# State-space prelude: both batches' x-projections before z, convolution taps read from PSUM, diagonals of both batches through DRAM, -|x| and an expert-block residual on VectorE

## What is computed

```
h = layernorm(x) * (1 + ca) + sa
xs, z = split(h @ in_proj.T)                       # 512 + 512 channels
xa = silu(conv4(xs) + conv_b)                      # causal, 4 taps
dt, Bc, Cc = split(xa @ x_proj.T)                  # 16 + 16 + 16
dt = softplus(dt @ dt_proj.T + dt_b)
for t: h_t = h_t-1 * exp(dt * A) + dt * B_t * xa   # 16 states a channel
       y_t = sum_n h_t[n] * C_t[n]
y = (y + xa * D) * silu(z)
x = x + ga * (y @ out_proj.T)
...
# layer 1, as the reference has it: the inner block adds its own input h
x = x + gb * (h + moe(rmsnorm(h)))
```

## Time and profile before

| | |
|---|---|
| Three runs, us | 2557.56, 2559.26, 2559.46; median 2559.26 |
| Profiled execution | 2562.03 us; its span 2560.2, granted clock of TensorE 0.957 of 2.4 GHz on average |
| TensorE, VectorE, ACT, POOL busy | 91%, 55%, 44%, 45% of the span |
| `mamba` begins | 34.7 us |
| First and last scan begin | 179.8, 530.1 us |
| `moe` of layer 1 begins | 2248.7 us |

### The profile page before, as it was taken

How to read it: one execution, slowest core, us unless ns; L and a number is a source line. 1 busy time by engine, 2 the same in 40 slices (tenths; PEclk the granted TensorE clock), 3 DMA queues, 4 the chain that set the end, 5 groups by cost and what they waited for, 6 DMA issues and landing times. The chain is left out here.

```text
span 2560.2 us, 34038 instructions
## 1 busy us (share of the span) xinstructions
PE 2337.4 (91%) x12526; PEld 1769.7 (69%) x12526; DVE 1416.2 (55%) x2477; ACT 1120.5 (44%) x1913; POOL 1140.2 (45%) x665
## 2 busy tenths in 40 slices
PE   6959999985999995999998989999999999949997
PEld 2329999983777764998896667777776777725554
DVE  5658888866222223545665875556556555463332
ACT  3467777722111112434433555546456464521221
POOL 0439999920332321433454445454545535223442
PEclk8969999997999997999998999999999999969999
DMA  6274181118412212000000100000000001055223
GB/s 243 83 284 114 58 329 59 64 73 267 133 30 34 32 26 98 1 1 1 1 1 19 56 1 19 15 10 19 1 23 1 19 9 34 1 175 145 45 42 64
DMA packets 108244, 168.30 MB, mean 66 GB/s; under 512 B 30482, under 2 KB 77586, under 8 KB 106004
## 3 DMA queue, kind: packets, MB, share of 16 engines
q1 hardware_dynamic: 93108, 145.35, 16.3%
q0 software_dynamic: 14976, 20.78, 5.1%
HBM read 115.94 MB, written 52.32 MB: 66 GB/s over the span
## 5 line engine op out<-in xcount | busy, mean ns | idle before, releaser
L638 POOL TENSOR_TENSOR mb_dbx<-mb_ud,mb_bb 128x1024 f32<-128x1024 f32 x128 | 302.0, 2363 | 57.2 <-DVE mb_h L496 41.7
L496 DVE TENSOR_TENSOR_SCAN mb_h<-ps,mb_dbx 128x1024 f32<-128x1024 f32 x128 | 292.2, 2289 | 47.9 <-ACT ps L608 37.5
L2298 PE MATMUL ps<-a_eT,a_v 128*128 128x512 f32 x576 | 297.2, 598 | 3.9 <-ACT a_eT L2175 3.9
L2131 POOL TENSOR_TENSOR a_e<-a_e,a_rc 128x1024 f32<-128x1024 f32 (+5 forms) x144 | 188.9, 1321 | 248.3 <-DVE a_rc L2047 247.9
L946 POOL DMA_INDIRECT e_acc<-e_hid,e_ids x78 | 123.6, 1585 | 370.8 <-DVE e_hid L1240 354.4
L2057 DVE TENSOR_REDUCE a_mx<-ps 128x1 f32<-128x1024 f32 (+7 forms) x256 | 192.7, 753 | 159.1 <-PE ps L2277 158.3
L2175 ACT ACTIVATE a_eT<-ps 128x512 f32<-128x512 f32 x288 | 171.1, 594 | 245.3 <-PE ps L2288 244.6
L740 PE MATMUL ps<-mb_dg,mb_hts 128*128 128x128 f32 x2048 | 251.2, 276 | 0.4
L740 PEld LDWEIGHTS ps<-mb_dg,mb_hts 128*128 128x128 f32 x2048 | 240.0, 193 | 1.9 <-issue 1.9
L1226 DVE COPY e_work<-ps 128x256 f32<-128x256 f32 x78 | 33.2, 425 | 356.4 <-PE ps L1064 356.4
L1803 POOL TENSOR_TENSOR a_elo<-a_e,a_ehi 128x1024 fp32r<-128x1024 f32 x48 | 117.6, 2451 | 223.2 <-ACT a_ehi L1656 117.7
(11 more groups left out here) (377 smaller groups left out, 5310.9 us busy)
## 6 DMA issues: line engine op xcount, KB each, us to landing
mb_bb<-mb_db_rows SPq DMA_DIRECT2D x16, 1024.0 KB, 12.6
mb_ddiag<-mb_dg SPq DMA_DIRECT2D x1, 8192.0 KB, 22.3
mb_dg<-mb_ddiag SPq DMA_DIRECT2D x8, 1024.0 KB, 14.0
e_wg<-in_g SPq DMA_DIRECT2D x8, 688.0 KB, 10.4
e_wu<-in_u SPq DMA_DIRECT2D x8, 688.0 KB, 10.7
e_wd<-in_d SPq DMA_DIRECT2D x8, 640.0 KB, 10.7
mb_dxa<-mb_bb SPq DMA_DIRECT2D x8, 512.0 KB, 2.6
mb_dz<-mb_xz SPq DMA_DIRECT2D x8, 512.0 KB, 2.9
```

Of the source, the lines that this page charges most:

```text
L496: dve.tensor_tensor_scan(h[:, at % 2, :], pair(at % 2), dbx[:, at % 2, :], 0.0, ALU.mult, ALU.add).then_inc(s_h, 1)
L638: pool.tensor_tensor(dbx[:, at % 2, :], ud[:, kk % 2, 0, :], bb[:, n, :], ALU.mult).then_inc(s_dbx, 1)
L2131: pool.tensor_tensor(probs(i, h), probs(i, h), rc[:, q:q + 1].to_broadcast([P, (i + 1) * P]), ALU.mult).then_inc(s["en"], 1)
L2298: mm = pe.matmul(ps[:, 6 + rows[u, i] % 2, :], v[:, j, u % 2, :], eT[:, k % ER, :], start=(j == 0), stop=(j == i))
```

## The change

In `mamba`:

- The order is now all eight x products (with `narrow` and `steps` as soon as they can), and only then all eight z products (`gated`, `gate`).
- `normalised` writes (x - mean) * rstd only, to two buffers. Scale and shift of the modulation go into the eviction to `hT`: TensorE transposes the 8 modulation blocks (`columns`, new), VectorE copies 8 columns to `modT`, ACT's Identity takes them as scale and bias.
- The zero-padded copy `xp` is gone. ACT's last tap and VectorE's three other taps read the product in PSUM, a tap that lies d tokens back over L - d elements.
- |v| is gone from ACT. VectorE computes relu r = max(v + b, 0) and then v - 2 r in a second pass; ACT's Exp adds the bias, which gives exp(-|v + b|).
- The step sizes and u of group 0 are made in `ud` itself, where the first scans read them.
- POOL builds no diagonals. `place_words` and `load_diag` run for both batches; SP issues batch 0's placements between the x spills.
- z is put in `xz`, `dbx`, `h` and again `xz`. So POOL's first product waits for the spill of z 2 and 3 (`s_zout[1]`), the first scan for z 4 and 5 (`s_zout[2]`), gate 6 for z 0 and 1.

In `moe` of layer 1, the four residual operations move from POOL to VectorE, behind the sixteen normalised tiles and the small constants and ahead of the wait for the router.

The core of the diff:

```diff
+        two = lambda area: area.rearrange("p a (t d) -> p (a t) d", d=D)
+        xn = [two(dg[:, 0:2, :]), two(dg[:, 4:6, :])]
+        hT = [dg[:, 2:4, :], bb[:, 12:14, :]]
+        zr = [xz[:, 0, :], xz[:, 1, :], dbx[:, 0, :], dbx[:, 1, :], h[:, 0, :], h[:, 1, :], xz[:, 0, :], xz[:, 1, :]]
...
             def load_ud(kk):
-                if kk >= 2:
+                if kk == 1:
+                    sp.wait_ge(s_low, BK)
+                    sp.wait_ge(s_uout[0], 16 * (CD - 1))
+                    sp.wait_ge(s_dtout[0], 16 * (CD - 1))
+                else:
...
+            for k in range(CD):
+                spill_xa(0, k)
+            spill_xa(1, 0)
+            spill_rows(0)
+            spill_xa(1, 1)
+            place_words(0)
+            spill_xa(1, 2)
+            spill_xa(1, 3)
+            sp.wait_ge(s_tr, 4)
+            sp.wait_ge(s_dgout, 16 * TB)
+            load_diag(0, 0)
+            spill_rows(1)
+            for k in range(1, CD):
+                spill_steps(0, k)
+                spill_z(k - 1)
+            spill_z(CD - 1)
...
             def conv(i):
...
+                    late = DC - 1 - tap
+                    ins = dve.scalar_tensor_tensor(xc[:, i % 2, late:L], pair(PAIR["x"][i])[:, 0:L - late], cw[:, k, tap:tap + 1],
+                                                   xc[:, i % 2, late:L], ALU.mult, ALU.add)
...
+            def relu(i):
+                dve.wait_ge(s_dt, i + 1)
+                own(dve.tensor_scalar(dtv[i // CD][i % CD], pair(PAIR["dt"][i]), db[:, i % CD:i % CD + 1], 0.0, ALU.add, ALU.max))
+                dve.scalar_tensor_tensor(low_v[i // CD][i % CD], dtv[i // CD][i % CD], -2.0, pair(PAIR["dt"][i]),
+                                         ALU.mult, ALU.add).then_inc(s_low, 1)
...
             for at in range(NIT):
                 kk, n = at // NS, at % NS
                 dve.wait_ge(s_da, at + 1)
                 dve.wait_ge(s_dbx, at + 1)
+                if at == 0:
+                    dve.wait_ge(s_zout[2], 32)
...
+            falling(0)
+            falling(1)
+            log1p(0)
+            for i in range(CD):
+                gate(i)
             log1p(1)
+            for i in range(CD, BK):
+                gate(i)
...
             pool.memset(zeros, 0.0).then_inc(s_zero, 1)
-            pool.wait_ge(s_ct, 1)
-            for n in range(NS):
-                if n == 12:
-                    pool.wait_ge(s_sp, CD)
-                pool.tensor_tensor(dg[:, n, :].rearrange("p (q c) -> p q c", q=TB), over(ident[:, :], TB),
-                                   spread(ct[:, n::NS], P), ALU.mult).then_inc(s_dg, 1)
             for at in range(NIT):
                 kk, n = at // NS, at % NS
-                if n == 0:
-                    pool.wait_ge(s_ud[kk % 2], 32 * (kk // 2 + 1))
+                if at == 0:
+                    pool.wait_ge(s_u, 1)
+                    pool.wait_ge(s_zout[1], 32)
...
+            columns()
             turned(0)
...
+            inner(0)
+            inner(1)
+            inner(2)
             turned(1)
+            inner(3)
+            inner(4)
+            narrow(0, 0)
+            narrow(0, 1)
+            inner(5)
+            narrow(0, 2)
+            narrow(0, 3)
+            inner(6)
+            steps(0)
...
+            for i in range(CD, BK):
+                steps(i)
+            for i in range(BK):
+                gated(i)
...
         def _(pool):
-            if hs is not None:
-                for r in range(NG // B, NG):
...
+            if hs is not None:
+                for r in range(NG // B, NG):
+                    four = slice(4 * r, 4 * r + 4)
+                    own(dve.tensor_tensor(res[:, four, :], hs[:, four, :],
+                                          over(mod[:, r // (NG // B), GB * D:(GB + 1) * D], 4), ALU.mult))
+                    ins = dve.tensor_tensor(x[:, four, :], x[:, four, :], res[:, four, :], ALU.add)
+                ins.then_inc(s_res, 1)
```

More of the change, by code:

```diff
@@ L473, in _ @@
-            relu(0, CD - 1)
-            split_xd(1)
-            for k in range(CD):
-                steps(0, k)
-            for k in range(CD):
-                relu(1, k)
-            for k in range(CD):
-                steps(1, k)
+            for i in range(6):
+                conv(i)
+            relu(0)
+            conv(6)
+            relu(1)
+            conv(7)
+            relu(2)
+            relu(3)
+            dve.wait_ge(s_dbl, 2)
+            dve.tensor_copy(xd[1], flat(ps[0:80, 2 * PAIR["narrow"][1]:2 * PAIR["narrow"][1] + 2, :])).then_inc(s_xd, 1)
@@ L555, in absolute @@
-            def absolute(b, k):
-                act.wait_ge(s_relu, b * CD + k + 1)
-                if b == 0 and k == 0:
-                    act.wait_ge(s_zfill, 16)
-                if b == 1 and k == 0:
-                    act.wait_ge(s_uout[0], 16 * CD)
-                act.activation(abs_v[b][:, k, :], pair(dt_pair(b, k)), ACT.Abs, bias=db[:, k:k + 1]).then_inc(s_abs, 1)
-            def falling(b):
-                for k in range(CD):
-                    act.wait_ge(s_abs, b * CD + k + 1)
-                    act.activation(abs_v[b][:, k, :], abs_v[b][:, k, :], ACT.Exp, scale=-1.0).then_inc(s_exp, 1)
@@ L582, in _, with activated @@
-            inner(1, 0)
-            for k in range(1, CD):
-                inner(1, k)
-                activated(1, k - 1)
-                absolute(0, k - 1)
-            activated(1, CD - 1)
-            gates(1, 0)
-            absolute(0, CD - 1)
+                act.activation(xc[:, i % 2, :], pair(PAIR["x"][i]), ACT.Identity, bias=cb[:, k:k + 1],
+                               scale=cw[:, k, DC - 1:DC]).then_inc(s_tap, 1)
+            def activated(i):
+                act.wait_ge(s_conv, i + 1)
+                act.activation(xa[i // CD][i % CD], xc[:, i % 2, :], ACT.Silu).then_inc(s_xa, 1)
@@ new lines, in falling, with log1p @@
+            def falling(b):
+                for i in range(b * CD, (b + 1) * CD):
+                    act.wait_ge(s_low, i + 1)
+                    act.activation(low_v[b][i % CD], low_v[b][i % CD], ACT.Exp, bias=db[:, i % CD:i % CD + 1]).then_inc(s_exp, 1)
+            def log1p(b):
+                for i in range(b * CD, (b + 1) * CD):
+                    act.wait_ge(s_exp, i + 1)
+                    act.activation(low_v[b][i % CD], low_v[b][i % CD], ACT.Ln, bias=1.0).then_inc(s_log, 1)
@@ new lines, in gate @@
+            def gate(i):
+                act.wait_ge(s_ip, BK + i + 1)
+                if i == 0:
+                    act.wait_ge(s_zfill, 16)
+                    act.wait_ge(s_xa, BK)
+                if i == 6:
+                    act.wait_ge(s_zout[0], 32)
+                act.activation(zr[i], pair(PAIR["z"][i]), ACT.Silu).then_inc(s_z, 1)
+            rows_of(0)
+            tap(0)
+            tap(1)
+            activated(0)
+            tap(2)
+            rows_of(1)
+            activated(1)
@@ L590, in _ @@
+            tap(3)
+            activated(2)
+            tap(4)
+            activated(3)
+            tap(5)
+            activated(4)
+            act.wait_ge(s_dbl, 1)
+            act.activation(xd[0], flat(ps[0:80, 2 * PAIR["narrow"][0]:2 * PAIR["narrow"][0] + 2, :]), ACT.Copy).then_inc(s_xd, 1)
+            tap(6)
+            activated(5)
+            tap(7)
+            activated(6)
+            activated(7)
             falling(0)
+            falling(1)
             log1p(0)
-            for k in range(1, CD):
-                gates(1, k)
@@ L709, in _ @@
[L709 to L716 removed]
+            inner(3)
[7 more added lines that the diff above has]
+            steps(0)
+            inner(7)
+            steps(1)
@@ L718, in turn_state @@
+            narrow(1, 0)
+            narrow(1, 1)
+            steps(2)
+            narrow(1, 2)
+            steps(3)
+            narrow(1, 3)
+            for i in range(CD, BK):
+                steps(i)
+            for i in range(BK):
+                gated(i)
+            pe.wait_ge(s_z, BK)
             def turn_state(at):
```

369 lines of the change are left out of this document (156 added, 213 removed).

## The result

The changed kernel took 2570.89 us (median of 7 runs, 2563.62 to 2574.76), the kernel before 2558.81 us (7 runs, 2556.67 to 2559.61): ratio **1.0041**, 95% interval 1.0031 to 1.0051. It is slower by 0.4%, where 2546.6 us was forecast. Three executions of 6161, 7607 and 8921 us (one of before beside e10, one each of e9 and e11) stand far outside all others and are left out of all medians and ratios.

A forecast was written before the change was run, and what follows sets the result against it. No engine binds the kernel throughout; the chain through the prelude to the first scan ends in compute. Gains 6.7 + 2.5 + 3.4 = 12.6 us off 2562.03 gave 2549.4 profiled, 2.8 lower as median: 2546.6 us, range 2539 to 2555.

The forecast's parts named there:

- (c): Batch 0's eight placements, now ahead of the scans: 5.1 us each, 40.9 us in all, done at 127.2.
- (e): First scans: 2.5 us gained as a POOL wait goes; batch 1's placements end near 250, step sizes needed at 261.
- (a): Start of the prelude: transposes start sooner, first product at 45.1 us against 47.17, a gain of 2 us.
- (b): Prelude up to the first C rows: first diagonal placement issued at 85.3 us.
- (d): Transfers behind the placements: 17.96 MB, first scan 45.9 us later at 173.1, 6.7 us earlier than before.
- (f): -|x| as two VectorE passes of 1.27 us a channel group: hidden under the transfers, else 10 us.
- (g): Residual operations at the second MoE block's start, off POOL: gain 3.4 us, with bounds 0 and 8.2.
- rival "slower": Batch 0's placements from a cold queue overlap less: 8.6 us each, first scan at 201, 2574.6 us; chance 7%.

The follow-up runs named there:

- e10: The changed kernel run again with nothing edited, on another chip: 2552.11 us, ratio 0.9967.
- e9: The changed kernel with batch 1's placed words going to a second, fresh DRAM array: 2552.44 us, ratio 0.9971.
- e11: e9 run once more, on the chip of e10: 2547.74 us, ratio 0.9954.
- e12: The changed kernel run a third time with nothing edited, on one more chip: 2562.57 us, ratio 1.0002.
- e13: e2's kernel run again, on the chip of e12: 2549.29 us, ratio 0.9956.
- e2: The changed kernel with batch 1's eight placements issued in parts of 3, 3 and 2 between later loads: 2552.23 us, ratio 0.9974.
- e3: The changed kernel with batch 1's placements taken out: 2551.54 us, ratio 0.9970.
- e1: The kernel before with only the four MoE residual operations moved from POOL to VectorE: 2557.35 us, ratio 0.9991.
- e6: The changed kernel with batch 1's placements split, SP's list up to the scans reordered and POOL issuing batch 0's placements: 2545.35 us, ratio 0.9952.
- e8: e6 with SP's rows, diagonals and spills put in the order of need: 2539.03 us, ratio 0.9920.
- e14: e8's kernel run again, beside e12 and e13: 2539.78 us, ratio 0.9912.

## Why the prediction was wrong

It failed on the sign in the first measurement, by two of its steps: (c) put a placement at 5.1 us, and it took 6.7; (e) put the wait for group 2's step sizes at nothing, and it was 14.0 us. The first makes the first scan 8.8 us later than forecast; with the wait that is 22.8 of the 23.0 us between the 2549.4 forecast for the profiled execution and its 2572.41. The first failure is a size, the second a term that was left out.

- **(a), (b) start and first C rows**: right. x product 0 starts at 45.10 (45.1), the first placement is issued at 84.12 (85.3).
- **(c) the placements, 5.1 us each**: mis-sized. They took 53.4 us to the last landing, 6.7 each, where 41.9 were forecast; that is 11.5 us, less the 1.2 by which they started sooner. The single row of before gave one pace for one execution, and I took it as the price. Over the eight traces of the table it ran from 5.0 to 6.7 us, and e10, e12 and e13 (44.3 to 45.6) are within 4 us of the forecast.
- **(d) the stream**: right in its size, 44.4 us behind the last placement against 45.9; the slices of 400 to 450 GB/s held, and the mean from 170 to 182 us was 415 GB/s. First scan 181.90 instead of 173.1, all of it from (c) (137.5 - 127.2 = 10.3, less the 1.5 of (d)). In e10, the same kernel, it is 173.97. Compute ended later than said, since gates 6 and 7 waited 9.7 us for the spills of z 0 and 1: decays at 157 instead of 147, POOL's first product at 161.5 instead of 152. Both stayed hidden under the transfers.
- **(e) first scans**: the 2.5 us came (347.8 us from first to last without the wait, against 350.3). But "Batch 1's placements reach the engines near 206, as now, and end near 250; the step sizes that queue behind them are needed at 261" is **the step that failed**. Three things in it were wrong. The placements now wait until batch 0's diagonals are loaded, and are *issued* 24 us behind the first scan (206.02 - 181.90, and 198.39 - 173.97 in e10); before they were issued at 186.62, 7 us behind it, beside the backlog. Step sizes behind them need another 15 to 18 us from the queue's being free to their landing (in the trace of before the second of the two tiles was issued at 240.83 and landed 8.5 us later, 15 us after the queue was free). And POOL needs them 83.8 us behind the first scan, not 88. So the wait is 24 + hold + 15 to 18 - 84: 24.1 + 55.4 + 18.3 - 83.8 = 14.0 in the first trace, 24.4 + 47.1 + 14.6 - 83.8 = 2.3 in e10. With the hold of before, 47.74, it would have come out near 3: this is what the oversight is worth at the pace of the forecast, and the other 11 us of the first trace are the slower words once more. In the traces with the eight in one piece the wait was 14.0, 8.2, 3.8, 2.4, 2.3 and twice 0, by hold and first scan. e2, e3 and e13 show that the order in SP's queue is its cause.
- **(f) -|x|**: right, last one done at 119.0 (118), under the transfers.
- **(g) MoE**: right, 3.5 us in the trace, 3.1 in e1 (3.4).

The rival "slower" had the right stretch (words from a cold queue overlap less), but at 8.6 us each and only in front of the first scan. With 6.7 there and 14 us at group 2 the kernel is slower without reaching the 7.3 us from which that rival was to decide. The first scan by itself costs 2.1 us; without the wait the same trace would give a span of about 2570.6 - 14.0 = 2556.6, 3.6 below before and no more than the spread behind the last scan.

On e10's chip the same prediction would have passed for right: 2552.11 us is inside its range, the traced execution took 2549.69 where 2549.4 was forecast, and the first scan is 0.9 us off. That the sum comes so close is partly luck, since the wait of (e) was missed there too and the stretch behind the last scan ran 5.1 us shorter than before where (g) gives 3.4.

What stays open: why the pace of single words differs, between chips and between executions on one chip. Place (e9, e11) was not shown to be it. None of the first measurement's 7 runs is below 2563.6, none of e10's 7 above 2556.0, which speaks for the chip; but e12's own runs span nearly both (2551.4 to 2564.5) on one chip, and which chip the first measurement had is not on record.

## What to carry to other kernels

When a change puts a step behind a new wait, work out three times for what is queued behind it: when the queue is free, when the load lands, and when it is needed after the change has moved that too. "As now" is a claim about each of them. A small scattered DMA belongs where nothing waits behind it: split between the urgent loads (shown by e2 and e13), or on the queue of an engine that is idle for as long as the issues take (e6's trace, not its median). And a duration from one execution of an operation that was off the critical path is a sample: before it goes onto the path, give it a range, and measure the kernel more than once and on more than one chip.

## What the runs showed of the hardware

- Eight DMAs of 2,048 words of 4 bytes took 39.8 to 53.4 us from first issue to last landing, with the 16 DMA engines busy 15% of the time while words alone passed (100 to 115 us of the first trace): 16,384 words, 2.4 to 3.3 ns each, for 64 KB. Half the words took 24.7 us.
- In rows of eight such a DMA held SP's queue 3.7 to 6.9 us; the last two of e2, by themselves, 2.3. Eight on POOL kept it 29.8, 29.6 and 32.1 us (e6, e8, e14), 21 to 24 of them in one stop before the eighth, and landed 36.8 us after the first issue in e6.
- Beside a POOL operation of 2.34 us, VectorE operations of 0.17 us took 2.19 to 2.35 us (before); with POOL idle 0.17 (e1).
- One kernel's place against another can change with the chip or the execution: before kept its time (medians 2558.4 to 2561.0 in all six measurements), the changed kernel had 2552.1, 2562.6 and 2570.9, and 13.1 us between the fastest and slowest of its 12 executions on one chip.
